# Attention loop: the gate's projection copied to SBUF, GpSimd's key work behind the score products, a new order on VectorE

## The reference

```python
q = l2norm((x @ Wq).reshape(Bb, Tt, H, K)) / np.sqrt(K)
k = l2norm((x @ Wk).reshape(Bb, Tt, H, K))
v = (x @ Wv).reshape(Bb, Tt, H, K)
gate = (x @ Wg).reshape(Bb, Tt, H, K)
...
P = jnp.where(strict, jnp.einsum('bhncd,bhnmd->bhncm', k_beta, k) * L, 0.0)
Ainv = jnp.eye(C, dtype=P.dtype) + P
...
v = Ainv @ v
k_cumdecay = Ainv @ (k_beta * jnp.exp(g)[..., None])

def step(S, inp):
    q_i, k_i, v_i, kcd_i, g_i, L_i = inp
    attn = jnp.where(tril, jnp.einsum('bhck,bhmk->bhcm', q_i, k_i) * L_i, 0.0)
    v_new = v_i - kcd_i @ S
    o_i = q_i * jnp.exp(g_i)[..., None] @ S + attn @ v_new
    g_last = g_i[..., -1:]
    S_new = S * jnp.exp(g_last)[..., None] + jnp.einsum('bhck,bhcd->bhkd', k_i * jnp.exp(g_last - g_i)[..., None], v_new)
    return (S_new, o_i)
...
o = o * jax.lax.rsqrt(jnp.mean(o * o, axis=-1, keepdims=True) + 1e-05) * norm_w
o = o * jax.nn.silu(gate)
return o.reshape(Bb, Tt, D) @ Wo
```

## Time and profile before

| | |
|---|---|
| median of 3 runs | 1187.23 us (1185.53 to 1190.21) |
| the profiled execution | 1186.16 us, span 1184.0 us |
| busy over the span | PE 1005.2, DVE 927.2, ACT 604.0, POOL 408.4 us |
| the attention's loop | from about 223 to about 790 us |
| mean granted clock of TensorE | 0.942 |

### The profile page before, as it was taken

The page is one execution under the profiler, slowest core; times in us unless marked ns, Lnnn a source line. Parts: engine busy times, 40 slices in busy tenths (PEclk is TensorE's granted clock), DMA queues, the critical chain, the costliest instruction groups (busy, mean ns, idle before and its releaser), DMA issues. The chain is left out here.

```text
span 1184.0 us, 38519 instructions
## 1 busy us (share of the span) xinstructions
PE 1005.2 (85%) x15510; PEld 721.5 (61%) x15510; DVE 927.2 (78%) x2432; ACT 604.0 (51%) x1614; POOL 408.4 (34%) x580
## 2 busy tenths in 40 slices
PE   2999977686898989989888887679999896799967
PEld 1888873354555555555565556558888774255546
DVE  3777646349999999999999999527776456899976
ACT  2433326444677777777777775654333262201144
POOL 2667540301221222222222221216665458500047
PEclk9999999788899999999999988879999888899989
DMA  9100005244544445444455543200000023945003
GB/s 251 32 2 1 1 1 174 55 89 100 110 97 107 105 94 110 103 84 105 105 111 111 111 93 76 44 2 1 2 1 1 11 65 87 282 116 170 1 19 125
DMA packets 282626, 93.31 MB, mean 79 GB/s; under 512 B 208977, under 2 KB 275409, under 8 KB 282449
## 3 DMA queue, kind: packets, MB, share of 16 engines
q1 hardware_dynamic: 247056, 84.03, 29.6%
q10 hardware_dynamic: 35392, 6.82, 3.0%
HBM read 56.20 MB, written 30.41 MB: 73 GB/s over the span
## 5 line engine op out<-in xcount | busy, mean ns | idle before, releaser
L1770 DVE TENSOR_TENSOR delta_tmp<-delta_PR 128x130 f32<-128x130 f32 (+12 forms) x416 | 156.4, 376 | 8.9
L1767 DVE TENSOR_TENSOR delta_PR<-delta_PR,delta_tmp 128x130 f32<-128x130 f32 (+12 forms) x416 | 152.5, 367 | 9.3
L1882 POOL TENSOR_TENSOR delta_S<-delta_E,delta_Bm 128x128 f32<-128x128 f32 x32 | 16.9, 527 | 265.3 <-issue 227.4
L1620 ACT ACTIVATE delta_y<-psum 32x128 f32<-32x128 f32 x256 | 68.7, 268 | 60.4 <-PE psum L1455 57.8
L506 POOL TENSOR_TENSOR ffn_H<-ffn_hid,ffn_H 128x512 fp32r<-128x512 f32 x48 | 61.8, 1293 | 57.0 <-DVE ffn_H L472 57.0
L506 POOL TENSOR_TENSOR first_H<-first_hid,first_H 128x512 fp32r<-128x512 f32 x48 | 61.7, 1290 | 52.9 <-DVE first_H L472 52.9
L1636 ACT ACTIVATE delta_wide<-delta_S 32x128 f32<-32x128 f32 x256 | 78.2, 306 | 3.2
L1405 PE MATMUL psum<-delta_MV,delta_KT 32*32 32x128 f32 x2048 | 66.2, 280 | 10.9 <-ACT delta_E L1570 10.9
L438 ACT ACTIVATE first_silu<-psum 128x512 f32<-128x512 f32 x48 | 28.8, 599 | 83.3 <-PE psum L391 83.3
L1421 PE MATMUL psum<-delta_T,delta_pad 128*32 128x128 f32 x2048 | 70.4, 295 | 0.9 <-issue 0.9
L1858 POOL TENSOR_TENSOR delta_VK<-delta_QK,both_eg 128x256 f32<-128x256 f32 x32 | 20.9, 655 | 145.4 <-DVE delta_QK L1703 145.3
(11 more groups left out here) (278 smaller groups left out, 2541.7 us busy)
## 6 DMA issues: line engine op xcount, KB each, us to landing
within_scratch<-delta_PT SPq DMA_DIRECT2D x128, 64.0 KB, 2.0
delta_PR<-within_scratch SPq DMA_DIRECT2D x16, 512.0 KB, 3.8
inverse_scratch<-delta_PR SPq DMA_DIRECT2D x16, 512.0 KB, 3.1
space_T<-taps_scratch SPq DMA_DIRECT2D x8, 1024.0 KB, 5.9
X<-taps_scratch SPq DMA_DIRECT2D x8, 1024.0 KB, 9.0
X<-in_x SPq DMA_DIRECT2D x32, 128.0 KB, 10.1
turned_scratch<-gates_XT SPq DMA_DIRECT2D x16, 256.0 KB, 2.3
delta_xT<-turned_scratch SPq DMA_DIRECT2D x32, 128.0 KB, 2.9
```

The source lines that it names most:

```text
L1620: i = a.activation(dst, heads(bank[6][rows, half * P:(half + 1) * P]), ACT.Copy)
L1767: i = v.tensor_tensor(after, after, t3, ALU.add)
L1770: i = v.tensor_tensor(t3, column.to_broadcast([P, j, n_after]), row.to_broadcast([P, j, n_after]), ALU.mult)
```

## The change

`sigmoid_g` is split. Its first `Exp` goes into a new step `keep_g`, which then copies the raw gate from PSUM to a new SBUF tile `raw_gate`; `keep_gate` on VectorE multiplies with this tile. The semaphore `p_v` is now given by this copy (values and gate both read), and TensorE's `project_vg` and `outputs` wait for `p_v` where they waited for `p_gate`. `widen(Z, 1)` comes ahead of `Ln` and the second `Exp`. On GpSimd, `middle_state` waits for VectorE's `new_state(Z, 0)` instead of its `own_heads(Z, 0)`; `fade_first` is done a slot ahead, and with `decayed_k` and `kept_k` it comes behind a wait for `within(n − 1)`. VectorE's order is rewritten: `new_state(Z, 0)` directly behind `own_heads(Z, 0)`, `add_o` and `new_stats` of the tile before behind it, and the solve steps dealt anew. `keys_out` and `keys_in` come one slot later.

```diff
 delta_sync
-        at(keys_out, n - 1)
-        at(keys_in, n - 2)
+        at(keys_out, n - 2)
+        at(keys_in, n - 3)
 delta_tensor, project_vg
-            pe.wait_ge(S.p_gate, t)
+            pe.wait_ge(S.p_v, t)
 delta_tensor, outputs
-            pe.wait_ge(S.p_gate, t + LAG_SCAN + 1)
+            pe.wait_ge(S.p_v, t + LAG_SCAN + 1)
 delta_scalar
-        a.activation(of_heads(M.VK[t % 6], 0), heads(bank[5][:, 0:DM]), ACT.Copy).then_inc(S.p_v, 1)
+        a.activation(of_heads(M.VK[t % 6], 0), heads(bank[5][:, 0:DM]), ACT.Copy)
-    def sigmoid_g(t):
+    def keep_g(t):
         gate = M.gate[t % 9]
         a.wait_ge(S.p_vg, t + 1)
         if t >= 9:
             a.wait_ge(S.o_gate, t - 8)
         own.seq(a.activation(gate, bank[5][:, DM:], ACT.Exp, scale=-1.0))
+        if t > 0:
+            a.wait_ge(S.p_gate, t)
+        a.activation(M.raw_gate, bank[5][:, DM:], ACT.Copy).then_inc(S.p_v, 1)
+
+    def sigmoid_g(t):
+        gate = M.gate[t % 9]
         own.seq(a.activation(gate, gate, ACT.Ln, bias=1.0))
         a.activation(gate, gate, ACT.Exp, scale=-1.0).then_inc(S.p_sig, 1)
...
         at(keep_v, n)
+        at(keep_g, n)
+        at(widen, Z, 1)
         at(sigmoid_g, n)
-        at(widen, Z, 1)
 delta_vector
-        v.tensor_tensor(gate, gate, bank[5][:, DM:], ALU.mult).then_inc(S.p_gate, 1)
+        v.tensor_tensor(gate, gate, M.raw_gate, ALU.mult).then_inc(S.p_gate, 1)
...
         at(own_heads, Z, 0)
-        solve(n, 0, 1)
         at(new_state, Z, 0)
-        solve(n, 1, 3)
+        at(add_o, O - 1)
         at(sum_qk, n)
-        solve(n, 3, 6)
+        if O - 1 < AHEAD * BLK:
+            at(new_stats, O - 1)
+        solve(n, 0, 4)
         at(faded_q, n - LAG_FORM)
-        solve(n, 6, 10)
+        solve(n, 4, 8)
         at(scale_qk, n)
-        solve(n, 10, 11)
+        solve(n, 8, 9)
         at(own_heads, Z, 1)
-        solve(n, 11, 12)
+        solve(n, 9, 10)
         at(new_state, Z, 1)
-        solve(n, 12, 13)
+        solve(n, 10, 17)
         at(keep_gate, n)
-        solve(n, 13, 21)
+        solve(n, 17, 22)
         at(sum_o, Z)
-        solve(n, 21, 24)
+        solve(n, 22, 25)
         at(keep_within, n - LAG_FORM)
-        solve(n, 24, 25)
+        solve(n, 25, 26)
         at(keep_attn, n - LAG_FORM)
-        solve(n, 25, 29)
+        solve(n, 26, 29)
         at(scale_o, Z)
-        at(add_o, O)
-        if O < AHEAD * BLK:
-            at(new_stats, O)
+    add_o(NT - 1)
 delta_gpsimd, middle_state
-        g.wait_ge(S.s_bm, 2 * t + 1)
+        g.wait_ge(S.s_x, 2 * t + 1)
...
-        at(fade_first, Z)
         at(middle_state, Z)
         at(fade_second, Z)
         at(gate_o, n - LAG_OUT)
+        if 0 < n <= NT:
+            g.wait_ge(S.f_kk, n)
+        at(fade_first, Z + 1)
         at(decayed_k, n)
         at(kept_k, n)
```

More of the change, by code:

```diff
@@ L1220, in delta_memory @@
     M.E, M.KT, M.MV = take("E", 512), take("KT", DM), take("MV", 1024)
+    M.raw_gate = take("raw_g", DM)
     M.QgT, M.AT, M.PT = some("QgT", 7, DM), some("AT", 6, 512), take("PT", 512)
```

## The result

The changed kernel takes 1193.68 us (median of 11 runs, 1190.77 to 1197.67), the kernel before beside it 1186.79 us (11 runs): a ratio of 1.0052, 95% interval 1.0035 to 1.0069, or + 6.2 us (6.9 by the two medians). That is just past the half per cent that I took as telling. The forecast was 1189.8, range 1177 to 1200.

The account below looks back on a forecast made before the run. VectorE was taken to bound the kernel (342 of 360 us busy). Pairs without statistics + 0.4 us, with them 0, slots 1 to 3 + 1.3, other partial slots + 0.9: + 2.6, so 1189.8 us, range 1177 to 1200.

Parts of the forecast that it names:

- the contention moves along the solve rather than off it: GpSimd's hold-ups of VectorE shift to other solve steps; nothing of the intended shift happens; the forecast case, chance 0.45.
- no change that a measurement can tell: Whole kernel: + 2.6 us to 1189.8, below the 0.5% (about 5.9 us) taken as telling; forecast case 1183 to 1193.
- The three signs that were to show it wrong: Wrong if decayed_k starts within half a microsecond of keep_within, short slots end with TensorE waited for, or TensorE's lower clock grows.
- state burst: GpSimd's middle_state, fade_second, gate_o at slot start: 0.48 us without statistics, 0.17 with, against 0.36: + 0.12 and − 0.19.
- key burst: GpSimd's key work and fade_first beside solve steps and sum_o: 0.45 us per slot against 0.61, − 0.16; bounds 0.05 and 0.75.
- GpSimd costs the solve more: Rival, slower: four full key-burst hits (0.75) and gate_o two (0.6), 24 × 0.45 = + 10.8 us, 1200.6 us; chance 0.20.
- Order: VectorE's new order: three more waits on the instruction directly ahead, each 0.115 us, + 0.35 us per full slot.
- Slots 1 to 3: No solve on VectorE covers ScalarE's gate copy while within waits for exp_decays: 0.42 × 3 = + 1.3 us.
- The other partial slots: Slots 4 to 7 and 32 to 35: one or two more neighbour waits in each, + 0.9 us.
- TensorE's clock: Danger sign, no size given: more of TensorE's time at its lower clock level, since its waits are gathered in one place.

Follow-up runs that it names:

- 2, hold on `within` alone: Kernel before with GpSimd's part alone (middle_state behind new_state, fade_first a slot ahead, key work behind within, keys_out and keys_in a slot later): 0.9986.
- 4, counted hold: Changed kernel with fade_first and key work held by a count of solve steps (two ahead of keep_within) instead of the end of within: 1180.02 us, 0.9945.
- 7, counted hold, order of before: Kernel before with GpSimd's part alone, key work held by the solve's step count instead of within; gate and VectorE's order as before: 0.9908, 10.9 us less.
- The fifth experiment: Changed kernel with key work held by step count, plus one solve step put back between own_heads(Z, 0) and new_state(Z, 0): 0.9887, against 0.9945 without that step.
- the ninth experiment: Changed kernel with project_qk computed twice in odd slots, 2 us more TensorE work with the same result: 1.0064.
- The eleventh: Kernel of the fifth experiment with project_qk computed twice in odd slots: 1171.36 us, 0.9846 against 0.9887.
- the eighth: Kernel before with the gate copy, GpSimd's part held by step count and keep_gate four solve steps later, VectorE's order otherwise as before: 0.9949, 6 us less.
- 10: Kernel of the eighth with project_qk computed twice in odd slots: 0.9895 against 0.9949.
- the first experiment: Kernel before with the gate copy alone (raw gate to SBUF, waits for p_v, widen ahead of Ln), GpSimd's and VectorE's order as before: 1.0142.

## Why the prediction was right, and where it was not

Right were what bounds the kernel and how the change works: the contention moves along the solve rather than off it. The time lies in the range, 3.9 us above the forecast. But the forecast was also "no change that a measurement can tell", with slower from 1193.2 us on, and 1193.68 is past that, in what had a chance of 0.24. And the 3.9 us are what is left of larger misses that partly cancel, which is luck.

The three signs that were to show it wrong all came, in some slots. The clock between 340 and 700 us was 0.95 instead of 0.99. Five short slots ended with VectorE waiting for TensorE's `to_state`, as five did before. And in the two short slots with the latest `within` the key work began within half a microsecond of `keep_within` (`decayed_k` at 544.93, `keep_within` at 545.02). Long slots took 17.2 to 17.5 us without statistics and mostly 17.5 to 17.9 with them (about 17.1 and 17.4 forecast), and TensorE's time went into waits for ScalarE's copy (51.8 us) more than for `own_heads` (11.0).

To size the terms I summed, over 16 slots, how much longer VectorE's solve steps, `new_state` and `keep_gate` took than the same instruction with GpSimd idle (us per slot):

| kernel | state burst | key burst | both | 25 slots | behind the loop |
|---|---|---|---|---|---|
| before | 0.36 | 0.62 | 0.98 | 397.4 | 403.8 |
| changed | 0.37 | 0.46 + 0.14 | 0.97 | 403.1 | 403.9 |
| 2, hold on `within` alone | 0.45 | 0.39 | 0.84 | 393.6 | 407.7 |
| 4, counted hold | 0.37 | 0.12 | 0.49 | 390.2 | 406.6 |
| 7, counted hold, order of before | 0.45 | 0.12 | 0.57 | 386.7 | 404.8 |

The last two columns are us of one profiled execution each: from the first `own_heads(Z, 0)` to the 26th, and from the 32nd, the last, to the end of the span. The 25 slots follow the contention: from the kernel before to 2 they lose 3.7 us (25 × 0.14 = 3.5), to 7 10.7 (25 × 0.41 = 10.3), and from the changed kernel to 4 12.9 (25 × 0.48 = 12.0, and 1.3 us less of waiting for `to_state`).

The 0.14 are the small steps of the last eliminations, 0.91 us per slot in the changed kernel and 0.77 before. In the other three kernels their means are those of before.

- **The key burst: the step that failed.** "0.45 us, against 0.61: − 0.16" was not there. Where the burst lies was right in most slots: from 516 us on `within` ended 9.8 us into the slot on average (9.2 forecast), and `decayed_k` came at 10.3, behind `fade_first`. Its price was not: 0.46 + 0.14 = 0.60 us, as much as before. I had counted `keep_gate` as clear of GpSimd; it loses 0.08 per slot on average. And I had not looked at the last eliminations. 24 slots × 0.16 = 3.8 us. The rival "GpSimd costs the solve more" had the right sign here, but its full price would have been 1200.6.
- **Order.** Forecast + 0.35 us per slot. Waits on the neighbour rose from 17.3 to 20.1 per slot (three expected), and the sum of all gaps and overlaps by 0.25 us; so 2.4 us less over 24 slots. The fifth experiment agrees with the price of 0.115 us itself. The Trainium skill's rule ("VectorE: DVE Perf Modes", The DRAIN you can't avoid), by which a semaphore on the neighbour costs nothing beyond the drain, would have made the fifth run equal to the fourth; the measurement decides against it.
- **State burst.** Forecast 0.48 without and 0.17 with statistics, the mean 0.32; measured about 0.5 and 0.24, the mean 0.37, so about + 1.1 us in all. One long step beside `gate_o`, as said.
- **Slots 1 to 3.** + 0.5 us measured over the three (from `sum_qk` to `sum_qk`, 24.83 and 25.36 us), + 1.3 forecast: − 0.8.
- **The other partial slots.** Forecast + 0.9 over slots 4 to 7 and 32 to 35. From the last of those three rows to the first scan slot the difference went from + 1.0 to − 0.3, and behind the 26th `own_heads(Z, 0)` it grew by 1.5: about + 0.2 in all, so − 0.7. Why slots 4 to 7 got shorter is open.
- **TensorE's clock.** Named as a danger, priced at nothing. Short slots without statistics took 14.43 to 14.74 us, but 15.12 and 15.15 where the clock was 0.89 and 0.79; one with statistics took 15.82 at 0.86 where others took 14.95. Over four such slots this is 2.3 us (0.9, 0.2, 0.6 and 0.6); before, short slots took 14.8 at 0.88 too. The first fence has three windows of 2 us at 364 us, the next one TensorE's timeline there and, for comparison, four matmuls of the same size at the full clock, the last one VectorE's timeline at the start of a later slot:

```profile
364.00:366.00 2.00, 0.15 (x1) 0.00 (x0) 1.90 (x6) 0.76 (x4) 0.00 (x0) 1.00 0.00 0
366.00:368.00 2.00, 1.19 (x35) 1.13 (x36) 2.00 (x7) 1.92 (x7) 0.00 (x0) 0.73 0.04 7
368.00:370.00 2.00, 2.00 (x6) 0.85 (x4) 1.90 (x7) 1.95 (x5) 0.00 (x0) 0.50 0.73 125
```
```profile
371.28 3.18 PE L1376 MATMUL psum<-both_w_in,delta_xT 128*128 128x512 f32 x4
...
560.22 1.98 PE L1366 MATMUL psum<-both_w_in,delta_xT 128*128 128x512 f32 x4
```
```profile
385.21 0.29 DVE L1785 TENSOR_TENSOR delta_Bm<-psum,consts 128x128 f32<-128x128 f32 x1 [1.05 <-PE psum L1469]
```

  TensorE did 0.15 us of work in the first window, with the clock at 1.00 (2.4 GHz). It then stands at 0.50 (1.2 GHz), and the projection ahead of `to_state` takes 3.18 instead of 1.98 us. At 385 us VectorE waits 1.05 us for `to_state`. In the ninth experiment the clock came back and only 1.9 us of the loop's 25 slots with it, and one short slot took 14.43 at 0.88, so the 2.3 us can't be called the clock's alone.

Together: 2.6 forecast + 3.8 + 2.3 + 1.1 − 0.8 − 2.4 − 0.7 = 5.9 us, and 0.5 that the profiled execution was late before the loop began (its first `sum_qk`, at 227.97 and 227.50 us), make 6.4, of 7.0 between the two profiled executions. The key burst is shown by experiments 4 and 7, and the order's price by 5; the other terms are readings of one execution each.

The second kernel's small gain has an answer in the table: the loop got shorter by what the contention says, and the stretch behind it took 3.9 us longer in that execution. The eleventh's short slots hardly differ from the fifth's but for three, which took 14.19, 13.91 and 13.90 instead of 14.83, 14.61 and 14.71 us, 2.1 us together (a fourth went from 14.17 to 14.52); of the 7.1 us between their profiled executions another 2.7 lie behind the loop.

Left open: why the stretch behind the loop, where no kernel changes anything, takes 403.8 to 408.9 us. The extremes go with TensorE's granted clock there (0.95 in the eleventh with 403.9, 0.92 in the eighth with 408.9), but 0.93 goes with 403.9 in the changed kernel and with 407.7 in the second. It bears on the copy's 5 us in 8: between the profiled executions of 7 and 8, 6.0 us apart, 2.5 lie in the 25 slots and 4.1 behind the loop. So how much of the copy's cost is the clock, which 10 gives back whole (6.4 us), and how much is another cost that happens to be of that size, stays open too.

## What to carry to other kernels

Work that contends with the busiest engine must be released by that engine's own progress (a count of its steps), not by the producer of the data it is meant to lie beside: here that producer ran 4 us ahead and more, and the gain of the ninth experiment moved it further. When an operand goes from PSUM to SBUF, the instruction that reads it becomes one that GpSimd can hold up (`keep_gate` went from 0.41 us to 0.62 at the same place in the first experiment). And parts of a change that are worth + 1.4%, + 5.9% and − 0.1% alone gave + 0.5% together, so measure each with what it needs, and price each neighbour pair on a saturated VectorE.

## What was not expected of the hardware

- Two microseconds of needless matmuls in every other slot made two kernels faster, by 0.54% and 0.41% (a third was not): with them TensorE's granted clock was 1.00 and 0.99 over the stretch instead of 0.94 and 0.97, and in the first all but one of the projections on the way to `to_state` took 1.98 us, where those of the eighth took up to 3.78.
- The price of a wait on the instruction directly ahead on VectorE is steady enough to be counted: 0.115 us from two rows gave 6.7 us, and 6.9 (4 to 10 by the intervals) were measured.
- A hold placed 4 us early is worth nothing that shows (1.0039 without it, 1.0052 with it, intervals overlapping), and placed right it is worth about 13 us. (In the run without it `kept_k` was late for another reason, so that run doesn't say what a burst wholly at its old place costs here.)
